# Four graph layers on one core: normalization, a mask and two additions move to GpSimd, ScalarE takes a copy from VectorE, and the target columns are spread by transposes

## The chip, the cores and the metric

The kernel runs on one core of a Trainium2 chip. The metric is the device time of one launch in microseconds; the profile is one execution of the program, and its clock column is the share of the full 2.4 GHz that TensorE was granted (0.5 is the 1.2 GHz level).

## The reference

The input is `x` (16 graphs of 512 nodes with 128 features) and `adj` (16 x 512 x 512 integers). Four layers follow each other, each of the form `x = x + layer(relu(layernorm(x)), adj)`.

```python
# layer 0: graph attention, one head
Wh = h @ W.T;  s1 = Wh @ a1;  s2 = Wh @ a2
e = where(adj == 0, -inf, leaky_relu(s1[:, None] + s2[None, :], 0.2))
att = where(adj == 0, 0, softmax(e));  out = att @ Wh
# layer 1: graph attention, four heads of 32 features, with a bias b
h = x @ W.T + b;  logits = leaky_relu(l_src[:, None] + l_dst[None, :], 0.2)   # per head
out = softmax(where(adj == 1, logits, -9e15)) @ h
# layer 2: alpha = sigmoid(where(adj == k, leaky_relu((h * a_k) @ h.T))), k = 1..4;  out = alpha @ h + bias
# layer 3: three steps of  m = h @ weight[i];  aggr = (adj != 0).T @ m;  h = gru_cell(aggr, h)
```

The layernorm has no scale or shift: `(x - mean) / sqrt(var + 1e-5)`.

## The kernel before

**Tiling and stages.** A graph is four chunks (`C = 4`) of 128 nodes. Rows lie on the partitions, so an attention row block is a tile of 128 x 512. The work of a graph is cut into steps of four lists: `A_STEPS` (layer 0), `L_STEPS` (layer 1 up to its probabilities), `B_STEPS` (the end of layer 1, and layer 2) and `C_STEPS` (layer 3). Each engine runs the steps of all 16 graphs in one order of its own. `in_order` sorts them by `BEGIN[stage][graph] + WHEN[engine][step]`, two tables of numbers written out in the file, so that stages of up to four graphs are interleaved on each engine. Inside an engine the order is fixed; between engines there are semaphores.

**Norms.** For each of four norms VectorE takes statistics (`stats`, `aggr`), and in `deviation_of` writes `minus_mean` (line 634) and `var_eps` (636, 638). GpSimd raises `var_eps` to the power -0.5 (`rstd`, line 363) and multiplies it with `minus_mean` (`shift`, 365). ScalarE applies both with a relu to each chunk (`norm`, line 394), and TensorE transposes the four chunks (`turn_rows`, 936) once all are there. ScalarE copies the transposed rows `hT` (399).

**Layer 0.** One 512-column product with `dst_rep` (the weight of the target term repeated over 128 columns) gives the target term of every node, spread over all partitions (`dst0`, 961). Four 1-column products give the source term (`src0`, 941), which VectorE scales into `s_lift` (682), and four of 128 columns give the values (`values0`, 941). All of them go through the same PSUM bank, `a_bank`, one after the other. VectorE makes the mask of 128 x 2048 (`mask0`, 678).

**Layer 1.** The same with four heads: `dst1` to `dst4` are 512-column products with `dst_rep` (1005), and the values and source terms come from four products of 132 columns (`values1`, 1013). VectorE adds the bias `b1_rows` on its way out of PSUM (739) and writes `s_lift` (741). For each of 16 head and chunk pairs VectorE takes a masked maximum (`n` steps, 642) and the logits (`v` steps, 663), ScalarE the exponential (460), TensorE four transposes (`q` steps, 948) and ScalarE their copy (468). After the aggregation (1040) VectorE scales the result (796) and adds it to `x1` (802).

**Queues.** GpSimd's queue issues the loads of `adj_h` and `edges`, SP's those of `x` and of the transposed adjacency, ScalarE's the store.

## Time and profile before

| | |
|---|---|
| median of 3 runs | 1065.93 us (1064.18 to 1067.51) |
| the profiled execution's own time | 1066.04 us |
| its span, from the first to the last instruction | 1063.9 us |
| granted clock, mean | 0.967 |
| TensorE matmul busy | 954.6 us, 90% of the span |
| VectorE busy | 892.3 us, 84% |
| ScalarE busy | 864.0 us, 81% |
| GpSimd busy | 132.6 us, 12% |

A share of busy time is a mean over the span, which has a fill of about 100 us at its start and a drain at its end in which one graph is alone. A matmul of fp32 operands has two records in the profile, a transpose has one.

### The profile page before, as it was taken

The numbers are of one execution on the slowest core, as the hardware profiler recorded it, in microseconds if no ns is written. First come the engines' busy times: TensorE is split into PE (matmuls) and PEld (weight loads), VectorE is DVE, ScalarE is ACT, GpSimd is POOL, SyncE is SP. The second block draws the span as 40 slices with busy tenths as digits, with TensorE's granted clock in tenths as the row PEclk, the third lists the DMA queues.
The fourth block names the chain that finished last, engine by engine and source line by source line (L and its number), as shares of the span: only waits on it lengthen the run. The fifth ranks groups of instructions, "written<-read, shape, count | busy, mean of one in ns | idle before, by whom it ended". The sixth has DMA issues, their size and how long they took to land.

```text
span 1063.9 us, 16086 instructions
## 1 busy us (share of the span) xinstructions
PE 954.6 (90%) x5024; PEld 609.6 (57%) x5024; DVE 892.3 (84%) x2710; ACT 864.0 (81%) x1860; POOL 132.6 (12%) x170
## 2 busy tenths in 40 slices
PE   4588998999989899999989899998989999998866
PEld 3455565666566566656556566656656665655443
DVE  5296989899898979899897989989897989979543
ACT  3367888979888897988888897988889798887742
POOL 1102011010202011020201201020201101010000
PEclk8558999999999999999999999999999999999989
DMA  2401204021210403121220402121030302111000
GB/s 72 109 1 39 72 11 109 11 61 52 68 51 14 106 11 77 44 60 51 56 64 10 110 11 60 60 61 51 15 105 11 79 31 61 50 40 51 1 11 10
DMA packets 42477, 52.32 MB, mean 49 GB/s; under 512 B 1296, under 2 KB 25872, under 8 KB 42384
## 3 DMA queue, kind: packets, MB, share of 16 engines
q0 software_dynamic: 16896, 25.17, 10.7%
q1 hardware_dynamic: 17040, 21.83, 6.5%
q10 hardware_dynamic: 8448, 4.20, 1.3%
q8 instruction: 44, 0.72, 0.3%
q14 instruction: 49, 0.40, 0.1%
HBM read 55.39 MB, written 4.19 MB: 56 GB/s over the span
## 4 chain that ended last, share of the span: by engine, by line
PE 52%; DVE 28%; ACT 10%; issue 6%; POOL 3%; DMA 0%; DVEq 0%; SPq 0%; ACTq 0%; POOLq 0%
PE l_bank L948 7%; DVE probs L642 6%; PE a_bank L981 6%; PE x_bank L1040 4%; PE a_bank L948 3%; PE h_bank L1102 3%; ACT hn L394 3%; PE r_bank L1102 3%; PE r_bank L1105 3%; DVE sess L843 3%; DVE sess L836 3%; PE h_bank L1105 3%; PE n_bank L1105 3%; DVE probs L663 3%; POOL rstd L363 2%
## 5 line engine op out<-in xcount | busy, mean ns | idle before, releaser
L663 DVE SCALAR_TENSOR_TENSOR probs<-spread,s_lift,probs 128x512 f32<-128x512 f32 x320 | 237.4, 747 | 4.0 <-DVE rmax L642 0.5
L642 DVE CUSTOM_DVE_ANT_0 probs<-spread,mask 128x512 f32<-128x512 f32 x320 | 211.8, 684 | 2.4 <-ACT spread L450 2.3
L363 POOL TENSOR_TENSOR rstd<-var_eps,power 128x4 f32<-128x4 f32 x64 | 88.0, 1375 | 882.5 <-DVE var_eps L636 603.0
L460 ACT ACTIVATE probs<-probs,shift_p 128x512 f32<-128x512 f32 x256 | 185.7, 725 | 5.7 <-DVE shift_p L659 5.7
L468 ACT ACTIVATE pT<-l_bank 128x512 f32<-128x512 f32 x256 | 151.8, 600 | 46.5 <-PE l_bank L948 46.3
L948 PEld LDWEIGHTS l_bank<-ident,probs 128*128 128x128 f32 x1024 | 124.3, 144 | 73.8 <-issue 46.0
L948 PE MATMUL l_bank<-ident,probs 128*128 128x128 f32 x1024 | 150.5, 278 | 6.1 <-ACT probs L460 5.1
L394 ACT ACTIVATE hn<-x,shift,rstd 128x128 f32<-128x128 f32 x192 | 80.5, 492 | 26.1 <-POOL shift L365 26.0
L1005 PE MATMUL l_bank<-hT,dst_rep 128*128 128x512 f32 x128 | 73.6, 658 | 12.1 <-ACT pT L468 8.5
L870 DVE SCALAR_TENSOR_TENSOR hid_n<-r_t,hid_n 128x512 f32<-128x512 f32 x48 | 33.1, 689 | 57.8 <-ACT r_t L518 57.8
L981 PE MATMUL a_bank<-values,pT 128*128 128x128 f32 x512 | 65.7, 286 | 0.7 <-ACT pT L428 0.7
L1088 PE MATMUL y_bank<-hn,sess 128*128 128x128 f32 x512 | 61.6, 278 | 4.2 <-DVE sess L843 4.1
L1088 PEld LDWEIGHTS y_bank<-hn,sess 128*128 128x128 f32 x512 | 58.4, 192 | 11.9 <-DVE sess L843 11.9
L981 PEld LDWEIGHTS a_bank<-values,pT 128*128 128x128 f32 x512 | 63.0, 202 | 2.0 <-ACT pT L428 2.0
L1040 PE MATMUL x_bank<-pT,values 128*32 128x512 f32 x512 | 58.2, 595 | 0.7 <-ACT pT L468 0.7
L450 ACT ACTIVATE spread<-l_bank 128x512 f32<-128x512 f32 x64 | 38.4, 600 | 23.4 <-PE l_bank L1005 23.4
L948 PEld LDWEIGHTS a_bank<-ident,probs 128*128 128x128 f32 x256 | 29.9, 149 | 44.5 <-ACT pT L428 35.8
L948 PE MATMUL a_bank<-ident,probs 128*128 128x128 f32 x256 | 44.4, 300 | 9.7 <-ACT probs L423 5.6
L460 ACT ACTIVATION_READ_ACCUMULATOR probs<-probs,shift_p 128x1 f32 x256 | 51.8, 202 | 0.0
L1105 PE MATMUL r_bank<-aggT,gi_w 128*128 128x512 f32 x96 | 49.4, 596 | 0.0
L1105 PE MATMUL h_bank<-aggT,gi_w 128*128 128x512 f32 x96 | 49.1, 593 | 0.0
L1105 PE MATMUL n_bank<-aggT,gi_w 128*128 128x512 f32 x96 | 49.1, 593 | 0.0
(175 smaller groups left out, 1956.5 us busy)
## 6 DMA issues: line engine op xcount, KB each, us to landing
adjt_i<-in_adj_t SPq DMA_DIRECT2D x16, 1024.0 KB, 5.2
edges<-in_adj POOLq DMA_DIRECT2D x16, 1024.0 KB, 5.9
adj_h<-in_adj POOLq DMA_DIRECT2D x16, 512.0 KB, 7.7
xin<-in_x SPq DMA_DIRECT2D x16, 256.0 KB, 2.9
out<-out_sb ACTq DMA_DIRECT2D x16, 256.0 KB, 3.8
weights_sb<-in_weights SPq DMA_DIRECT2D x1, 840.0 KB, 4.7
```

The source lines that it names most:

```text
L363: g.tensor_tensor(rstd[n][:], var_eps[n][:], power[:], op=ALU.pow).then_inc(pool_step[n], 1)
L394: s.activation(hn[n][:, c, :], rows[:, c, :], ACT.Relu, bias=shift[n][:, c:c + 1], scale=rstd[n][:, c:c + 1]).then_inc(hn_ready[n], 1)
L460: s.activation(row, row, ACT.Exp, bias=shift_p[:, head, c:c + 1], accum_out=den[:, head, c:c + 1]).then_inc(probs_ready, 1)
L468: s.activation(pT[:, head - 1, :, c * P:(c + 1) * P], l_banks[unit % 2][:, :].rearrange("p (j i) -> p j i", j=C), ACT.Copy).then_inc(pT_co ...
L642: return v.tensor_tensor_reduce(out=row, in0=spread_row, in1=mask, scale=1.0 / LIFT, scalar=-3e38, op0=ALU.subtract, op1=ALU.max, accum_ou ...
L663: v.scalar_tensor_tensor(row, spread_row, source, row, ALU.min, ALU.subtract, reverse1=True).then_inc(ready, 1)
L948: last = t.transpose(dst[:, j * P:(j + 1) * P], row[:, j * P:(j + 1) * P], ident[:])
L981: last = t.matmul(a_bank[:, c * P:(c + 1) * P], pT0[:, j, c * P:(c + 1) * P], values0[:, j, :], start=(j == 0), stop=(j == C - 1))
L1005: t.matmul(l_banks[head % 2][:, :], dst_rep[:, head, :], hT[1][:, :], start=True, stop=True).then_inc(dst_ready, 1)
L1040: last = t.matmul(x_bank[h * HD:(h + 1) * HD, :], values1[:, j, h * HD:(h + 1) * HD], pT[:, h, j, :], start=(j == 0), stop=(j == C - 1), s ...
L1088: last = t.matmul(y_bank[:, c * P:(c + 1) * P], sess[:, j, c * P:(c + 1) * P], hn[2][:, j, :], start=False, stop=(j == C - 1), skip_group_ ...
L1105: t.matmul(bank[:, :], gi_w[:, layer, gate * D:(gate + 1) * D], aggT[:, :], start=start, stop=True).then_inc(gi_ready, 1)
```

## The change

What it does, part by part:

- **Norms.** `minus_mean` and `shift` go. GpSimd writes each normalized chunk itself, `(x - mean) * rstd`, in sixteen instructions per graph of 128 x 128. The relu moves into the readers: ScalarE's copy of `hT`, ScalarE's `state_hi`, VectorE's `split`. For layer 2, whose product reads the rows untransposed, GpSimd runs one pass more over the 512 columns (`ramp2`), and the product waits for it. TensorE's transposes wait for one chunk at a time.
- **Layer 0.** The source and target terms become columns 128 and 129 of the values (`values0_w`, 130 columns). Four times 130 don't fit into a bank, so three chunks are multiplied and copied (`values0`), then the fourth (`last0`). The target column is then spread over the partitions by four transposes of the column repeated 128 times (`spread_column`) in place of the product with `dst_rep`. The order in `a_bank` becomes rows, values, last, dst. GpSimd makes the mask in four parts of 512 columns.
- **Layer 1.** `values1_w` has 136 columns (values, four source and four target terms). ScalarE copies them from PSUM in two instructions of 272 columns. VectorE adds a constant to the 16 source columns. `dst1` to `dst4` are `spread_column` too, and come after `values1`. The bias isn't added to the values any more: GpSimd adds it to `x1` after the norm has read that (`plus1`, 512 columns).
- **x2.** GpSimd adds `x1` to the scaled result (512 columns), between VectorE's `scaled` and `stats2`.
- **hTa.** ScalarE makes it from `hT` in SBUF in place of the PSUM bank.
- **Orders.** `BEGIN` and `WHEN` hold other numbers, so each engine has another order of steps. The distance between two graphs in `BEGIN` goes from about 6,780 to about 6,270.
- **GpSimd's queue.** The load of the next graph's `adj_h` now also waits for the mask parts of the graph before, and the mask parts stand behind that load.

```diff
-A_STEPS = (... + [f"norm0_{c}" for c in range(4)] + ["rows0", "mask0", "dst0", "src0", "values0"] + ...
+A_STEPS = (... + [f"norm0_{c}" for c in range(4)] + [f"mask0_{c}" for c in range(4)] + ["rows0", "values0", "last0", "dst0"] + ...
...
+    COLS0, COLS1 = D + 2, D + 2 * H1
+    SOURCE1, TARGET1 = D, D + H1
...
-                pool.wait_ge(pool_step[n], p.count(1, 1))
-                g.tensor_tensor(shift[n][:], minus_mean[n][:], rstd[n][:], op=ALU.mult).then_inc(ln_ready[n], 1)
+            def norm(p, n, c, rows):
+                if c == 0:
+                    pool.wait_ge(pool_step[n], p.count(1, 1))
+                    if p.before().exists():
+                        pool.wait_ge(hT_ready[n], p.before().count(1, 1))
+                g.tensor_scalar(hn[n][:, c, :], rows[:, c, :], moments[n][:, c, 0:1], rstd[n][:, c:c + 1],
+                                op0=ALU.subtract, op1=ALU.mult).then_inc(hn_ready[n], 1)
...
             def load_adj(p):
                 if p.before().exists():
+                    pool.wait_ge(mask0_ready, p.before().count(C, C))
...
+            def mask_of(p, c):
+                pool.wait_ge(adj_loaded, p.count(16, 16))
+                if p.before().exists():
+                    pool.wait_ge(logits0_ready, p.before().count(C, c + 1))
+                g.tensor_scalar(mask0[:, c, :], adj_h[:, c, :], 0.0, MASK, ALU.is_equal,
+                                ALU.mult).then_inc(mask0_ready, 1)
+            def plus_b1(p):
+                pool.wait_ge(hn_ready[1], p.count(C, C))
...
+                g.tensor_tensor(row, row, b1_rows[:, :].unsqueeze(1).to_broadcast([P, C, D]),
+                                op=ALU.add).then_inc(plus1_ready, 1)
...
+                if step == "x2":
+                    pool.wait_ge(scaled_ready, p.count(1, 1))
+                    pool.wait_ge(plus1_ready, p.count(1, 1))
+                    g.tensor_tensor(x2[:, :, :], x1[:, p.graph % 2, :, :], x2[:, :, :], op=ALU.add).then_inc(x2_ready, 1)
...
+                if step == "ramp2":
+                    pool.wait_ge(hT_ready[2], p.count(1, 1))
+                    g.tensor_scalar(hn[2][:, :, :], hn[2][:, :, :], 0.0, None, op0=ALU.max).then_inc(ramp_done, 1)
...
-                s.activation(hT[n][:, :], src[:, :], ACT.Copy).then_inc(hT_copied[n], 1)
+                s.activation(hT[n][:, :], src[:, :], ACT.Relu).then_inc(hT_copied[n], 1)
...
+                elif step == "last0":
+                    act.wait_ge(last0_ready, p.count(1, 1))
+                    s.activation(values0[:, C - 1, :], a_bank[:, 0:COLS0], ACT.Copy).then_inc(last0_copied, 1)
...
+                elif step == "values1":
+                    act.wait_ge(val1_ready, p.count(1, 1))
+                    if prev.exists():
+                        act.wait_ge(l1_done, prev.count(1, 1))
+                    for half in range(2):
+                        s.activation(values1[:, 2 * half:2 * half + 2, :].rearrange("p c k -> p (c k)"),
+                                     l_banks[half][:, 0:2 * COLS1], ACT.Copy).then_inc(val1_copied, 1)
...
-                        v.tensor_tensor(values1[:, pair, :], both[:, :, 0:D],
-                                        b1_rows[:, :].unsqueeze(1).to_broadcast([P, 2, D]), ALU.add)
+                    v.tensor_tensor(sources1[:, :, :], values1[:, :, SOURCE1:SOURCE1 + H1],
+                                    source_const[:, :].unsqueeze(1).to_broadcast([P, C, H1]),
+                                    ALU.add).then_inc(src1_copied, 1)
...
             def turn_rows(p, n, dst):
-                pe.wait_ge(hn_ready[n], p.count(C, C))
                 for c in range(C):
+                    pe.wait_ge(hn_ready[n], p.count(C, c + 1))
                     last = t.transpose(dst[:, c * P:(c + 1) * P], hn[n][:, c, :], ident[:])
...
+            def spread_column(dst, columns, k, ready):
                 for c in range(C):
+                    last = t.transpose(dst[:, c * P:(c + 1) * P], columns[:, c, k:k + 1].to_broadcast([P, P]), ident[:])
+                last.then_inc(ready, 1)
...
-                    t.matmul(l_banks[head % 2][:, :], dst_rep[:, head, :], hT[1][:, :], start=True,
-                             stop=True).then_inc(dst_ready, 1)
+                    spread_column(l_banks[head % 2], values1, TARGET1 + head - 1, dst_ready)
```

## Rows read from the trace of the kernel before

**Rows 1.** Stretches of the span: busy us of each engine, TensorE's clock, DMA.
```profile
149.49:757.01 607.52, 574.04 (x3135) 367.29 (x3138) 550.70 (x1672) 535.42 (x1161) 84.28 (x100) 1.00 0.20 53
...
106.00:172.00 66.00, 62.69 (x332) 39.29 (x331) 60.13 (x180) 59.10 (x130) 8.03 (x10) 1.00 0.24 60
964.00:1000.00 36.00, 30.68 (x171) 18.86 (x172) 26.41 (x68) 27.05 (x60) 1.75 (x2) 1.00 0.13 37
```

**Rows 2.** TensorE's waits, 149.49 to 757.01 us: total, times, longest.
```profile
PE a_bank L941 <- DVE s_lift L682: 13.6, 10, 1.4
PE x_bank L936 <- ACT hn L394: 8.9, 12, 0.8
```

**Rows 3.** The chain that ended last, 309.71 to 311.86 us: start, us, work.
```profile
309.71 0.86 PE r_bank L1102 x2
...
311.43 0.44 PE l_bank L948 x4
```

**Rows 4.** TensorE's groups, same ten periods: busy us, mean ns | idle before.
```profile
L948 PE MATMUL l_bank<-ident,probs 128*128 128x128 f32 x640 | 91.2, 273 | 0.2 <-ACT probs L460 0.2
...
L1005 PE MATMUL l_bank<-hT,dst_rep 128*128 128x512 f32 x80 | 43.1, 621 | 6.0 <-ACT pT L468 6.0
...
L961 PE MATMUL a_bank<-hT,dst_rep 128*128 128x512 f32 x20 | 10.2, 593 | 0.0
...
L941 PE MATMUL a_bank<-src_w,hT 128*128 128x1 f32 x80 | 9.5, 240 | 0.0
```

**Rows 5.** VectorE's groups that the change touches, same ten periods.
```profile
L739 DVE TENSOR_TENSOR values<-l_bank,b_rows 128x256 f32<-128x256 f32 x20 | 8.2, 413 | 0.0
...
L802 DVE TENSOR_TENSOR x<-x 128x512 f32<-128x512 f32 x10 | 6.9, 690 | 0.3
...
L678 DVE TENSOR_SCALAR mask<-adj_h 128x2048 bf16<-128x2048 bf16 x10 | 6.8, 684 | 0.0
...
L634 DVE TENSOR_SCALAR minus_mean<-moments 128x4 f32<-128x4 f32 x40 | 6.7, 167 | 0.7
```

**Rows 6.** ScalarE's groups: two of the ten periods, one of the whole span.
```profile
L394 ACT ACTIVATE hn<-x,shift,rstd 128x128 f32<-128x128 f32 x121 | 50.7, 493 | 3.4 <-POOL shift L365 3.3
...
L450 ACT ACTIVATE spread<-l_bank 128x512 f32<-128x512 f32 x40 | 24.1, 602 | 9.0 <-PE l_bank L1005 9.0
...
L535 ACT ACTIVATE gi_w<-r_bank 128x384 f32<-128x384 f32 x1 | 0.5, 491 | 0.7 <-PE r_bank L931 0.7
```

**Rows 7.** GpSimd's groups, whole span.
```profile
L365 POOL TENSOR_TENSOR shift<-minus_mean,rstd 128x4 f32<-128x4 f32 x64 | 19.4, 303 | 5.0
...
L358 POOL TENSOR_SCALAR_AFFINE_SELECT ident<-ident 128x128 f32<-128x128 f32 x1 | 0.3, 287 | 0.2 <-POOL ones_h L356 0.2
L352 POOL MEMSET ones<- 128x128 f32 x1 | 0.2, 205 | 0.3 <-POOLq L1175 0.3
...
L355 POOL MEMSET minus_half<- 128x1 f32 x1 | 0.1, 96 | 0.0
```

**Rows 8.** The power operation (ns least/median/most), one of them, VectorE beside it.
```profile
L363 POOL TENSOR_TENSOR rstd<-var_eps,power x64: 1007/1380/2586, 5.3 to 1022.5; 128x4 f32<-128x4 f32 x64
...
524.31 1.38 POOL L363 TENSOR_TENSOR rstd<-var_eps,power 128x4 f32<-128x4 f32 x1 [6.25 <-DVE var_eps L636]
...
524.14 0.68 DVE L642 CUSTOM_DVE_ANT_0 probs<-spread,mask 128x512 f32<-128x512 f32 x1
...
524.75 0.69 DVE L642 CUSTOM_DVE_ANT_0 probs<-spread,mask 128x512 f32<-128x512 f32 x1
```

**Rows 9.** VectorE's groups with two SBUF inputs, ten periods, first and last.
```profile
L663 DVE SCALAR_TENSOR_TENSOR probs<-spread,s_lift,probs 128x512 f32<-128x512 f32 x200 | 148.3, 747 | 2.5 <-DVE rmax L642 0.5
L642 DVE CUSTOM_DVE_ANT_0 probs<-spread,mask 128x512 f32<-128x512 f32 x200 | 132.2, 683 | 0.1
...
L836 DVE SCALAR_TENSOR_TENSOR sess<-sess 128x512 f32<-128x512 f32 x40 | 25.9, 686 | 0.3 <-ACT sess L488 0.2
...
L865 DVE TENSOR_TENSOR state_lo<-hn,state_hi 128x512 fp32r<-128x512 f32 x10 | 6.8, 684 | 0.0
```

More of the change, by code:

```diff
@@ L20 @@
 PLAIN = 1024.0
[L23 removed]
+A_STEPS = (["stats0", "aggr0", "mean0"] + [f"norm0_{c}" for c in range(4)] + [f"mask0_{c}" for c in range(4)] + ["rows0", "values0", "last0", "dst0"] + [f"m{c}" for c in range(4)]
            + ["u0", "top0", "u1", "t0", "below0", "u2", "t1", "max0", "u3", "t2", "t3", "den0", "rden0"] + [f"sum0_{c}" for c in range(4)] + ["x1"])
[L25 removed]
+L_STEPS = (["stats1", "aggr1", "mean1"] + [f"norm1_{c}" for c in range(4)] + ["plus1", "count", "rows1", "mask1", "edges", "values1", "dst1"]
            + [f"n{c}" for c in range(4)] + ["dst2"]
@@ L31 @@
 B_STEPS = ([f"sum1_{j}" for j in range(4)] + ["den1", "scaled", "x2", "stats2", "aggr2", "mean2"]
-           + [f"norm2_{c}" for c in range(4)] + ["rows2"] + [f"z{n}" for n in range(4)] + ["kinds"]
+           + [f"norm2_{c}" for c in range(4)] + ["rows2", "ramp2"] + [f"z{n}" for n in range(4)] + ["kinds"]
            + [f"s{n}" for n in range(4)] + [f"w{n}" for n in range(4)] + ["x3", "stats3", "aggr3", "mean3"]
@@ L220, in graph_layers @@
         moments = [sb(f"moments{n}", [P, C, 2]) for n in range(NORMS)]
-        var_eps, rstd, minus_mean, shift = ([sb(f"{m}{n}", [P, C]) for n in range(NORMS)]
-                                            for m in ("var_eps", "rstd", "minus_mean", "shift"))
+        var_eps, rstd = ([sb(f"{m}{n}", [P, C]) for n in range(NORMS)] for m in ("var_eps", "rstd"))
         cell = [sb(f"cell{n}", [P, 1]) for n in range(NORMS)]
@@ L280, in graph_layers @@
         pool_step = [sem(f"pool_step{n}") for n in range(NORMS)]
-        ln_ready = [sem(f"ln_ready{n}") for n in range(NORMS)]
         hn_ready = [sem(f"hn_ready{n}") for n in range(NORMS)]
@@ L381, in step_of @@
                     deviation(p, int(step[4]))
+                if step[:5] == "norm0":
+                    norm(p, 0, int(step[6]), xin[:, p.graph % 2, :, :])
+                if step[:5] == "norm1":
+                    norm(p, 1, int(step[6]), x1[:, p.graph % 2, :, :])
+                if step[:5] == "norm2":
+                    if step == "norm2_0" and p.before().exists():
+                        pool.wait_ge(av2_done, p.before().count(1, 1))
+                    norm(p, 2, int(step[6]), x2)
+                if step == "ramp2":
+                    pool.wait_ge(hT_ready[2], p.count(1, 1))
+                    g.tensor_scalar(hn[2][:, :, :], hn[2][:, :, :], 0.0, None, op0=ALU.max).then_inc(ramp_done, 1)
+                if step[:5] == "norm3":
+                    if step == "norm3_0" and p.before().exists():
+                        pool.wait_ge(rest_ready, p.before().count(LAYERS, 1))
+                    norm(p, 3, int(step[6]), x3)
             load_adj(Place(0))
@@ L432, in step_l @@
                 prev = p.before()
-                if step[:5] == "norm1":
-                    norm(p, 1, int(step[6]), x1[:, p.graph % 2, :, :])
-                elif step == "rows1":
+                if step == "rows1":
                     copy_hT(p, 1, l_bank0)
```

194 lines of the change are left out of this document (80 added, 114 removed), and 118 rows, old and new, of the table WHEN.

## The prediction

> **What bounds the kernel now.** The split of the span into stretches comes first [rows 1]. Ten whole periods lie between the starts of two layer 1 aggregations, at 149.49 and 757.01 us, so one graph takes 607.52 / 10 = 60.75 us. Of these TensorE is busy 57.40, VectorE 55.07, ScalarE 53.54 and GpSimd 8.43. Three engines are close to full; the reader is to see that TensorE has 3.35 us of room per graph, VectorE 5.68, and that the granted clock is 1.00 there (the 2.4 GHz level). Outside the window the kernel fills and drains.
>
> What TensorE waits for is in the table of waits of the same window [rows 2]: 13.6 us over ten graphs for the `s_lift` column of layer 0, 8.9 for normalized rows from ScalarE, the most of 33.5 us in all. So little is handed over, the rest is TensorE's own work: it is the first bound. VectorE at 91% is the second, and so near that relief for one alone would soon meet the other.
>
> **TensorE's part of the change.** The chain that ended last [rows 3] prices what is swapped. In the chain a 512-column matmul advances TensorE by 0.86 us (two passes, each a record), four transposes by 0.44 us when nothing holds them. The busy columns give the same order [rows 4]: a 512-wide `dst` product is 43.1 / 40 = 1.08 us in layer 1 and 10.2 / 10 = 1.02 in layer 0, four transposes 91.2 / 160 = 0.57. The change replaces five such products per graph (4.31 + 1.02 = 5.33 us) by five sets of four transposes of a repeated column. No row shows a repeated column as an input; bounds are 0.44 (the chain) and 1.08 (no gain), and I take 0.57, the row of the same operation: 2.85. It also drops the four source products of layer 0, 0.95 us. `values0` grows from 128 to 130 columns and `values1` from 132 to 136, in four products each: 24 columns at 0.86 us for 512, +0.04. Sum: 57.40 - 5.33 - 0.95 + 2.85 + 0.04 = 54.0, or 3.4 less per graph.
>
> The 1.36 us per graph that TensorE waits before `values0` goes with the source column. In its place come two waits of the same kind, on the copies before `last0` and before the `dst0` transposes, each behind a ScalarE copy of about 0.5 us. In TensorE's new order, as the tables sort it, `rows2`, `z0` and `q0` stand between `values0` and `last0`, and `z1` to `z3` and `q1` between `last0` and `dst0`, which covers them; but with ScalarE and VectorE nearer to each other other waits will come, and I keep the idle time at 3.35.
>
> **VectorE's part.** Per graph it loses [rows 5] the layer 0 mask 0.68, the layer 1 bias additions 0.82, the addition of x2 0.69, and seven small instructions of the size of `minus_mean`, 0.167 each (four of these, three of `s_lift`): 1.17. Such small ones advance the engine by less than they last, so 0.5 is the lower end of that term. It gains a 16-column addition, 0.17. Sum 3.36 - 0.17 = 3.2: 51.9 us. The split step changes from one two-input form to another of the same width: nothing.
>
> **ScalarE's part.** The norms take 50.7 / 121 = 0.42 us each [rows 6], sixteen of them 6.7 per graph. It gains two copies of 272 columns: 384 columns took 0.491 and 512 took 0.60, 0.85 ns per column, so 0.40 each and 0.79 together; the last copy of 130 columns is 0.28 by the same line, and `values0` with 390 columns saves 0.10. 53.54 - 6.7 + 0.97 = 47.8. It falls behind and is cover from now on.
>
> **GpSimd's part.** No row has such an operation at this width, so each is bounded [rows 7]. A 128-column write took 0.205 us and a 1-column one about 0.10; a 128-column pass with one input took 0.287. Sixteen norms of 128 columns lie between 0.205 and ScalarE's own 0.49; I take 0.29: 4.6 us. A 512-column pass with one input is 0.10 + 4 x 0.105 = 0.52 to 0.10 + 4 x 0.187 = 0.85; I take 0.6: four mask parts 2.4, `ramp2` (four times as wide in all, 512 columns) 0.6. Additions of 512 columns with two inputs lie between VectorE's 0.69 and 2 x 0.85 = 1.7; I take 1.2, twice 2.4. New work 10.0 us, less the four `shift` products of 0.3: GpSimd goes from 8.4 to about 17 of 60 us and is no bound by itself. The Trainium skill (GPSIMD Engine Reference, section Elementwise) gives about 2.6 cycles per element at 1.2 GHz for a two-input addition; an estimate by it is 1.1 us for 512 columns. No row here shows one, and by it the sum of new work would be 9.8.
>
> **What the new work meets.** This decides. The power operation, with two four-column inputs, took between 1.007 and 2.586 us, 1.380 in the median [rows 8]. One of the median length was issued at 524.31, just after a VectorE instruction with two SBUF inputs (spread and mask) had begun at 524.14 to last to 524.82. That its 0.37 us above the shortest ends about there says that GpSimd's reads were kept out until that instruction let go, and 2.586 that they can be kept out for two. The reverse doesn't show: VectorE's next one starts at 524.75, 0.61 after the last. But four-column reads are over at once, and those of the new work aren't. VectorE's instructions with two SBUF inputs are [rows 9] 148.3 + 132.2 us in the two softmax forms and 141 in eight further groups (the first 25.9, the last 6.8): 422 in 607.5 us, 69% of the time. If every GpSimd read of the new work holds VectorE for its whole duration, VectorE loses 10.0 x 0.69 = 6.9 us per graph; if none does, 0. A 128-column GpSimd write takes 0.1 us beyond its start, half of its duration; I take half as held, 3.5 us: VectorE at 51.9 + 3.5 = 55.4.
>
> **Sum.** The busier engine is then VectorE with 55.4 (TensorE 54.0), much as it was TensorE with 57.4 (VectorE 55.1), and I keep that idle of 3.35: 58.8 us per graph, 2.0 less. The stretch from 106 to 1000 us is worked at about this pace (its first and last windows still have TensorE busy for 62.69 of 66 and 30.68 of 36 us [rows 1]): 894 / 60.75 = 14.7 periods. In the fill and the drain one graph is alone; there a norm loses 0.30 of `shift` and four times 0.42 of ScalarE [rows 6, 7] and gains four times 0.29, while x2 costs 0.5 more and the first graph has one copy more: nothing on balance, 3 us either way. 14.7 x 2.0 = 29 us. The profiled execution's own time is 1066.04 for a span of 1063.9, and the median of the runs is 1065.93, the same within 0.1: 1066 - 29 = 1037 us.
>
> **Rivals.**
> 1. VectorE isn't held at all (the short reads slip into its gaps, as those of the power operation do). TensorE bounds again: 54.0 + 3.35 = 57.35, 3.4 less, 14.7 x 3.4 = 50: 1016 us. For it: VectorE's starts beside GpSimd today. Against: those reads are of four elements. Chance 0.24.
> 2. The other side: each GpSimd operation holds VectorE for its whole duration. VectorE 51.9 + 6.9 = 58.8, plus 3.35 is 62.2, 1.4 more than now: 1066 + 21 = 1087 us. With two-input additions at their upper bound of 1.7 it is 1097. It decides from the point where VectorE passes 57.4, a loss of 5.5 us per graph, 0.55 us for each us of new GpSimd work. For it: the durations of 1.38 and 2.59 us show that the two engines do exclude each other. Against: VectorE waits 5.7 us per graph anyway, and part of the loss falls there. The Trainium skill (SBUF, section Who interferes with whom) states this rule outright: the shared pair is held for the full instruction and the other blocks. This trace shows the block in one direction only. Chance 0.24.
> 3. The norms come late: kept out one VectorE instruction each, four take 4 x (0.68 + 0.29) = 3.9 us in place of 0.30 + 1.68 = 2.0, and x2 is 1.2 later; TensorE, in order, stands at the transposes of `rows2` and `rows3`. That is 2 x 1.9 + 1.2 = 5.0 us per graph, of which half beyond cover gives 54.0 + 3.35 + 2.5 = 59.9: 0.9 less, 1053 us. For it: TensorE waits 0.89 us per graph there already [rows 2]. Against: it now starts with the first norm. Chance 0.10.
> 4. The change doesn't cheapen the spreading (a repeated column costs a full product): TensorE 54.0 + 2.5 = 56.5, period 59.9 again, 1053 us. Nothing speaks for it but the missing row. Chance 0.04.
>
> **Numbers.** The forecast has 0.38, with its own range of 1024 to 1052. Within 0.3% (3 us, about what a measurement of this kernel tells from no change) lies only the seam between the forecast and rival 2: 0.06, taken from these two. Faster: 0.24 + 0.10 + 0.04 + 0.34 = 0.72; slower 0.22. Down to 1008 (rival 1 with transposes at 0.44) and up to 1086, with half of rival 2 beyond it, the range leaves out about 2 in 10.
>
> **What would show it.** Right: the sets of transposes for `dst` at about 0.57 us; TensorE at 54 and ScalarE at 48 us per period; GpSimd at 17 or more with waits in its durations; the softmax instructions of VectorE longer in the mean than 747 and 684 ns, or with gaps, by 3.5 us per graph in sum. Rival 1: these means unchanged and TensorE at 94% busy. Rival 2: VectorE at 58 us or more per period. Rival 3: VectorE and TensorE both under 90%, with waits on `hn` from GpSimd. Wrong in size it would be if a norm on GpSimd takes 0.5 us or more, or if the bound moves to GpSimd's queue, where mask parts wait for a load issued shortly before them.

## The result, and the profile after

The changed kernel takes 1203.2 us in the median of four runs (1202.1 to 1203.3), the kernel before 1065.1 beside it (1063.4 to 1067.5): 1.129 times as long, with a 95% interval of 1.127 to 1.132. The forecast was 1037, faster. The time lies outside the range, and past the rival of the other side (1087) too.

The page of the changed kernel, with the share of busy time, TensorE's clock and GpSimd's use in 40 slices:

```profile
span 1201.5 us, 16247 instructions
...
PE 982.3 (82%) x5056; PEld 638.3 (53%) x5056; DVE 901.4 (75%) x2545; ACT 788.7 (66%) x1652; POOL 579.9 (48%) x474
...
POOL 4427375482727547272753717365472727532120
PEclk8567898999988899998989989898999989898989
```

The longer span isn't filled with work. TensorE has 982.3 us of it and is idle for 219, where before it had 954.6 and was idle for 109. VectorE and ScalarE are idle too. No engine is a bound by its own work. GpSimd's row repeats: slices at 10 to 40% stand between slices at 50 to 90%, so its work comes in bursts.

Ten whole periods again, between the starts of two layer 1 aggregations (busy of TensorE, its weight loads, VectorE, ScalarE, GpSimd; clock, DMA share, GB/s), and in them TensorE's waits that answer to [rows 2] (total, times, longest):

```profile
160.46:859.38 698.92, 593.09 (x3152) 385.93 (x3151) 559.64 (x1575) 489.81 (x1031) 368.46 (x290) 0.94 0.18 46
```

```profile
PE x_bank L941 <- POOL hn L356: 57.4, 68, 3.4
...
PE a_bank L941 <- POOL hn L356: 2.6, 3, 0.9
```

A period is 69.9 us, where [rows 1] had 60.75. Of the 9.1 more, 1.9 are in TensorE's busy time (59.3 after 57.4) and 7.2 in its idle time (10.6 after 3.35). Waits for normalized rows are 6.0 us per graph; they were 0.89. VectorE at 56.0 and ScalarE at 49.0 are where the prediction had them (55.4 and 47.8).

GpSimd's groups over the whole span (busy, mean ns | idle before), and least, median and most of the two costliest:

```profile
L356 POOL TENSOR_SCALAR hn<-x,moments,rstd 128x128 f32<-128x128 f32 x192 | 197.1, 1037 | 6.9 <-issue 5.0
L370 POOL TENSOR_SCALAR mask<-adj_h 128x512 bf16<-128x512 bf16 x64 | 146.7, 2314 | 83.1 <-DMA adj_h<-in_adj 83.1
...
L408 POOL TENSOR_SCALAR hn<-hn 128x512 f32<-128x512 f32 x16 | 25.5, 1597 | 0.8 <-PE x_bank L941 0.5
L378 POOL TENSOR_TENSOR x<-x,b_rows 128x512 f32<-128x512 f32 x16 | 21.6, 1352 | 1.3
L385 POOL TENSOR_TENSOR x<-x 128x512 f32<-128x512 f32 x16 | 20.7, 1291 | 35.7 <-DVE x L804 35.7
```

```profile
L356 POOL TENSOR_SCALAR hn<-x,moments,rstd x192: 784/878/1942, 40.3 to 1162.1; 128x128 f32<-128x128 f32 x192
```

```profile
L370 POOL TENSOR_SCALAR mask<-adj_h x64: 1915/2248/3184, 9.9 to 1028.4; 128x512 bf16<-128x512 bf16 x64
```

None of these is near its price, the additions apart. A norm chunk takes 784 ns at least and 1037 in the mean, where 0.29 us was taken and 0.49 was the upper bound. A mask part takes 1915 at least against 0.6. The relu pass takes 1.6 us, and is one input with one operation, yet slower than the additions of two inputs.

What this does is to be seen on GpSimd's own timeline (start, us, work):

```profile
647.39 1.03 POOL L348 TENSOR_TENSOR rstd<-var_eps,power 128x4 f32<-128x4 f32 x1 [22.89 <-DVE var_eps L656]
648.53 3.20 POOL L356 TENSOR_SCALAR hn<-x,moments,rstd 128x128 f32<-128x128 f32 x4
651.82 1.29 POOL L378 TENSOR_TENSOR x<-x,b_rows 128x512 f32<-128x512 f32 x1
653.07 1.47 POOL L348 TENSOR_TENSOR rstd<-var_eps,power 128x4 f32<-128x4 f32 x1
654.64 3.67 POOL L356 TENSOR_SCALAR hn<-xin,moments,rstd 128x128 f32<-128x128 f32 x4
658.29 1.26 POOL L385 TENSOR_TENSOR x<-x 128x512 f32<-128x512 f32 x1
661.16 1.51 POOL L348 TENSOR_TENSOR rstd<-var_eps,power 128x4 f32<-128x4 f32 x1 [1.61 <-DVE var_eps L656]
662.84 4.56 POOL L356 TENSOR_SCALAR hn<-x,moments,rstd 128x128 f32<-128x128 f32 x4 [0.17 <-issue]
667.35 0.86 POOL L395 DMA_DIRECT2D edges<-in_adj  x1
668.21 0.75 POOL L364 DMA_DIRECT2D adj_h<-in_adj  x1
668.97 1.59 POOL L408 TENSOR_SCALAR hn<-hn 128x512 f32<-128x512 f32 x1
```

Three power operations start within 14 us, and the engine waits for 1.6 of the 23.2 us. Norm 2's power is made from 661.16 on; its fourth chunk is ready at 667.40, 6.2 us later. Before, power, shift and four chunks on ScalarE took 1.38 + 0.30 + 4 x 0.42 = 3.4 us [rows 6 to 8]. Then the layer 2 product waits for the relu pass, which stands behind two load issues and ends at 670.56.

The VectorE and TensorE groups that the forecast named:

```profile
L662 DVE CUSTOM_DVE_ANT_0 probs<-spread,mask 128x512 f32<-128x512 f32 x320 | 218.1, 702 | 11.4 <-ACT spread L434 7.0 <-ACT spread L481 3.7
L686 DVE SCALAR_TENSOR_TENSOR probs<-spread,sources,probs 128x512 f32<-128x512 f32 x256 | 194.6, 764 | 3.1
...
L946 PE MATMUL l_bank<-ident,values 128*128 128x128 f32 x256 | 41.4, 291 | 5.3 <-DVE other_kinds L754 2.9 <-ACT pT L499 2.4
```

Least, median and most of the masked maximum, in the changed kernel and before:

```profile
L662 DVE CUSTOM_DVE_ANT_0 probs<-spread,mask x320: 675/685/1093, 16.9 to 1111.8; 128x512 f32<-128x512 f32 x160
```

```profile
L642 DVE CUSTOM_DVE_ANT_0 probs<-spread,mask x320: 654/684/693, 18.0 to 981.2; 128x512 f32<-128x512 f32 x160
```

In the mean the masked maximum went from 684 to 702 ns and the logits from 747 to 764. The longest masked maximum takes 0.41 us more than the median, and the shortest norm chunk on GpSimd takes 0.78: no masked maximum was lengthened by a whole GpSimd instruction. A set of four transposes for `dst` costs 41.4 / 64 = 0.65 us of TensorE, close to the 0.57 taken.

### The profile page after: what moved, and what is told of

It is laid out like the page before. It is cut to its first block and busy times, and to the rows that moved or that the text cites. A ratio compares the mean times of both kernels' runs of the same rounds, so it can differ in the third digit from the quotient of the medians.

```text
span 1201.5 us, 16247 instructions
## 1 busy us (share of the span) xinstructions
PE 982.3 (82%) x5056; PEld 638.3 (53%) x5056; DVE 901.4 (75%) x2545; ACT 788.7 (66%) x1652; POOL 579.9 (48%) x474
## 5 line engine op out<-in xcount | busy, mean ns | idle before, releaser
L356 POOL TENSOR_SCALAR hn<-x,moments,rstd 128x128 f32<-128x128 f32 x192 | 197.1, 1037 | 6.9 <-issue 5.0
L686 DVE SCALAR_TENSOR_TENSOR probs<-spread,sources,probs 128x512 f32<-128x512 f32 x256 | 194.6, 764 | 3.1
L951 PE MATMUL l_bank<-ident,probs 128*128 128x128 f32 x1024 | 164.8, 291 | 32.2 <-ACT probs L491 30.8
L370 POOL TENSOR_SCALAR mask<-adj_h 128x512 bf16<-128x512 bf16 x64 | 146.7, 2314 | 83.1 <-DMA adj_h<-in_adj 83.1
L941 PE MATMUL x_bank<-ident,hn 128*128 128x128 f32 x128 | 48.6, 386 | 93.5 <-POOL hn L356 93.5
L941 PEld LDWEIGHTS x_bank<-ident,hn 128*128 128x128 f32 x128 | 20.2, 158 | 123.9 <-POOL hn L356 122.8
L1093 PEld LDWEIGHTS y_bank<-hn,sess 128*128 128x128 f32 x512 | 60.4, 191 | 24.3 <-DVE sess L848 24.2
L884 DVE SCALAR_TENSOR_TENSOR keep<-z_t,state 128x512 f32<-128x512 f32 x32 | 26.6, 831 | 44.2 <-ACT z_t L546 44.2
L356 POOL TENSOR_SCALAR hn<-xin,moments,rstd 128x128 f32<-128x128 f32 x64 | 57.5, 910 | 1.7
L644 DVE BATCH_NORM_STATS2 stats<-x 128x6 f32<-128x128 f32 x192 | 41.8, 281 | 18.7 <-POOL x L385 17.9
L535 ACT ACTIVATE aggT<-n_bank 128x512 f32<-128x512 f32 x32 | 19.1, 597 | 54.5 <-PE n_bank L1125 54.5
```

The costliest lines, as they stand in the source:

```text
L356: g.tensor_scalar(hn[n][:, c, :], rows[:, c, :], moments[n][:, c, 0:1], rstd[n][:, c:c + 1], op0=ALU.subtract, op1=ALU.mult).then_inc(hn_r ...
L370: g.tensor_scalar(mask0[:, c, :], adj_h[:, c, :], 0.0, MASK, ALU.is_equal, ALU.mult).then_inc(mask0_ready, 1)
L686: v.scalar_tensor_tensor(row, spread_row, source, row, ALU.min, ALU.subtract, reverse1=True).then_inc(ready, 1)
L941: last = t.transpose(dst[:, c * P:(c + 1) * P], hn[n][:, c, :], ident[:])
L951: last = t.transpose(dst[:, j * P:(j + 1) * P], row[:, j * P:(j + 1) * P], ident[:])
L1093: last = t.matmul(y_bank[:, c * P:(c + 1) * P], sess[:, j, c * P:(c + 1) * P], hn[2][:, j, :], start=False, stop=(j == C - 1), skip_group_ ...
```

## The experiments

Each median stands with its ratio to the kernel before, run beside it, and the 95% interval. Before each run two or more outcomes were written down, with a time for each. In nine of the eighteen (e1, e2, e3, e4, e7, e9, e10, e12, e15) the time fell outside all of them, in e3 and e15 by under 3 us.

### Undoing parts of the changed kernel

Five kernels keep the change and its new orders, and move work back. `ON_ACT` lists the norms that ScalarE makes as before.

```diff
+ON_ACT = (0, 1, 2, 3)      # e1;  (2, 3) in e2
+                if n in ON_ACT:
+                    pool.wait_ge(pool_step[n], p.count(1, 1))
+                    g.tensor_tensor(shift[n][:], minus_mean[n][:], rstd[n][:], op=ALU.mult).then_inc(ln_ready[n], 1)
+                    return
...
-                g.tensor_scalar(mask0[:, c, :], adj_h[:, c, :], 0.0, MASK, ALU.is_equal,      # e3
+                        v.tensor_scalar(mask0[:, :, :], adj_h[:, :, :], 0.0, MASK, ALU.is_equal,
```

> The changed kernel with all sixteen norm instructions per graph back on ScalarE (shift on GpSimd and minus_mean on VectorE again, no ramp2), placed in ScalarE's order just before the copy of the rows (layer 0's before the copy of layer 1's values of the graph before); everything else as changed. Late results (the chains wait for slow GpSimd instructions, 0.8 to 2 us for each norm where 0.29 was priced): 187 us lie between the measured 1203 and the 1016 that TensorE's own work would give, and most of it goes: 1030 to 1080 us. Held VectorE (each GpSimd instruction blocks VectorE's two-input ones): the norms are 255 of GpSimd's 580 busy us, so 40 to 45% of the 187 goes: about 1120 us, and VectorE's mean durations fall only in part.

> The changed kernel with only the norms of layers 2 and 3 back on ScalarE, those whose rows TensorE waits for in the changed kernel (93.5 us before the transposes into x_bank); layers 0 and 1 stay on GpSimd. Late results: nearly all of what moving all four back gives, within 15 us of it. Held VectorE: half of what moving all four back gives.

> The changed kernel with layer 0's mask back on VectorE, one instruction of 0.69 us just before the first masked maximum; the norms stay on GpSimd. The four mask parts take 9 us of GpSimd's queue per graph and wait for a load (83 us in all), with a later norm behind them. Late results through GpSimd's queue: 20 to 70 us faster than the changed kernel, 1135 to 1185. Late results through each norm's own length alone: no change or slower, 1200 to 1215, for VectorE has 11 us more. Held VectorE: 147 of 580 busy us go, so about a quarter of 187: 1155 us, with VectorE's mean durations back halfway.

Measured: all norms back 1184.0 us (1.111 [1.108, 1.114]), norms 2 and 3 alone back 1149.8 (1.082 [1.078, 1.086]), the mask back 1197.5 (1.124 [1.120, 1.128]). Norms 2 and 3 are worth 53 us; moving 0 and 1 as well takes 34 of them away again. The mask, a quarter of GpSimd's busy time, is worth 6, and the two intervals overlap. So in this kernel the amount of GpSimd work costs less than which results come late. That with all norms back 119 us stay was more than either expectation had, and called for the next two, in which mask, norms and x2 are back and only the bias addition stays on GpSimd (in e6 norms 0 and 1 too).

> The changed kernel's orders with nearly all of the GpSimd work back: norms on ScalarE, layer 0's mask and the last addition of x2 on VectorE; the bias addition stays on GpSimd, the transposes of repeated columns and ScalarE's copy of the values stay. If slow GpSimd work alone makes the loss (1150 us with the norms of layers 2 and 3 back): 1010 to 1060 us. If the new orders are bad in themselves, fitted to durations that the chip doesn't have: still above 1110 us.

> As the run before, but the norms of layers 0 and 1 stay on GpSimd, where nothing was seen to wait long for them. Slow GpSimd work alone: 1020 to 1080 us. Bad orders: above 1110 us, and within 30 us of the run with all four norms back, or faster than it, as the norms of layers 0 and 1 on ScalarE cost 34 us with these orders (1184 against 1150).

Measured: 1178.8 (1.106 [1.102, 1.109]) and 1136.3 (1.066 [1.063, 1.070]). With nearly all work back, e5 is still 113 us above the kernel before, and it is slower than e6, which has more moved. The new orders don't fit work that isn't where they were made for.

### The orders

The changed kernel's computation in the old tables, each new step in the place of the one that it replaces (`values0`, `last0`, `dst0` for `dst0`, `src0`, `values0`; `values1` ahead of `dst1`).

```diff
-BEGIN, WHEN = ...   # the tables of the changed kernel
+BEGIN, WHEN = ...   # the tables of the kernel before
+NEW = {"mask0": [], "dst0": ["values0"], "src0": ["last0"], "values0": ["dst0"], "dst1": [],
+       "values1": ["values1", "dst1"]}
```

> The same work as the first kernel of this job, in the order of the kernel before on every engine: each step where it stood, layer 1's values now in the place of its first target product and that one in the place of the values, layer 0's values, last chunk and target column in the places of target, source and values; the bias addition on GpSimd before the load of the edges. So only TensorE's part, the copy of the values by ScalarE and the bias on GpSimd are new. If TensorE's work bounds as it did, at 54.0 us per graph in place of 57.4: 1015 to 1045 us. If the orders matter little: within 15 us of the first kernel of this job.

> All work as changed (norms, mask parts, both additions and ramp2 on GpSimd), in the order of the kernel before: norms right behind their power operation, x2 before mean2, the mask parts behind ramp2 of two graphs before and the load. If the new orders make most of the loss: below 1130 us. If slow GpSimd work makes it: 1180 to 1260 us, since these orders were made without it.

Measured: e7, with norms, mask and x2 back, 1103.8 (1.034 [1.028, 1.040]); e8, with all work moved, 1208.4 (1.134 [1.128, 1.140]). The new tables are worth 5 us with the work moved, where the two intervals overlap, and cost 75 with it back. They are no cause of the loss; the work that moved costs 105 us in the old tables (e8 less e7). What is left in e7, 38 us, is the cheaper way to spread the target columns, with ScalarE's copies, the relu in the readers and the bias addition on GpSimd. TensorE's waits there, whole span:

```profile
PE a_bank L1057 <- ACT values L539: 34.9, 16, 2.7
PE l_bank L1057 <- DVE other_kinds L861: 21.7, 16, 2.2
```

TensorE now stands behind copies that ScalarE makes, 2.2 us per graph in layer 0, where the `s_lift` wait that went was 1.2 per graph over the whole span. In layer 1 it stands 1.4 us per graph before the first target column, which needs the copied values and a count from VectorE. That is so in the old tables. In the changed kernel, with its own tables, the two waits of layer 0 are almost gone (whole span):

```profile
PE a_bank L970 <- ACT values L439: 0.6, 1, 0.6
```

```profile
PE a_bank L946 <- ACT values L443: 0.4, 1, 0.4
```

### The kernel before, with one part of the change

```diff
 e9_old_dst234
-                    t.matmul(l_banks[head % 2][:, :], dst_rep[:, head, :], hT[1][:, :], start=True,
+                    if head > 1:
+                        spread_column(l_banks[head % 2], values1, D + head - 1, dst_ready)
 e11_old_layer0
+SLOTS = {"tensor": {"dst0": ["values0"], "src0": ["last0"], "values0": ["dst0"]},
+         "scalar": {"dst0": ["values0"], "src0": [], "values0": ["last0", "dst0"]}}
 e10_old_norms_pool (in e14_old_norms23_pool for n = 2, 3 alone)
-                g.tensor_tensor(shift[n][:], minus_mean[n][:], rstd[n][:], op=ALU.mult).then_inc(ln_ready[n], 1)
+                for c in range(C):
+                    g.tensor_scalar(hn[n][:, c, :], rows[:, c, :], moments[n][:, c, 0:1], rstd[n][:, c:c + 1],
+                                    op0=ALU.subtract, op1=ALU.mult).then_inc(hn_ready[n], 1)
 e12_old_mask_pool
+                for c in range(C):
+                    g.tensor_scalar(mask0[:, c, :], adj_h[:, c, :], 0.0, MASK, ALU.is_equal, ALU.mult)
```

> The kernel before with one part alone: layer 1's target columns 2 to 4 spread by four transposes each instead of a 512-column product (136-column values, the additions of VectorE 132 columns wide instead of 128); the first head keeps its product, no order changes, and no step waits for more than before. If the price of the transposes holds (0.57 us a set against 1.08) and TensorE is the bound: 3 x 0.5 = 1.5 us per graph, 1040 to 1050 us. If TensorE's clock falls as it waits more and takes the saving back: 1055 to 1068 us, with a mean clock below 0.967.

> The kernel before with one part alone: all norms on GpSimd (128-column instructions right behind the power operation, relu in the readers, ramp2), orders unchanged. A norm then takes 4 x 0.8 to 1.0 us in place of 0.3 + 1.7, at four places per graph, 1.5 to 2.5 us later each. Late results: 2 or 3 of the places are waited for, 5 us per graph: 1110 to 1150 us. If the GpSimd work were hidden behind other work: 1055 to 1075 us.

> The kernel before with one part alone: layer 0's values with 130 columns in two goes, the last chunk and the spreading of the target column behind them in the same bank, in the slots of the old target, source and value products. The serial use of the bank makes TensorE wait for a copy of about 0.5 us before the last chunk and 0.3 before the transposes: in the run with all work back in the old orders it waited 34.9 us in all for that. If these waits set the time: 1075 to 1100 us. If TensorE's saved products (1.0 us for the target, 0.95 for the sources, less 0.57) win: 1045 to 1060 us.

> The kernel before with one part alone: layer 0's mask in four parts on GpSimd, right behind the load of adj_h, orders unchanged. GpSimd was idle there for 18 us and the parts take 9 after 6 of the load. Nobody waits for them: what is left is what they hold VectorE, 9 us of GpSimd reading per graph: with the 80 us that 460 us of unawaited GpSimd work cost, 147 us of it cost 25 less 11 saved on VectorE: 1070 to 1085 us. If VectorE is held only by norm-like instructions: 1055 to 1066 us.

> The kernel before with only the norms of layers 2 and 3 (and ramp2) on GpSimd, orders unchanged. If the lateness of these two, whose rows TensorE and ScalarE wait for, makes most of the 88 us: 1125 to 1150 us. If each norm's GpSimd time costs alike through VectorE: half of it, about 1110 us.

| run | median, us | ratio and interval |
|---|---|---|
| e9, heads 2 to 4 spread by transposes | 1074.9 | 1.009 [1.007, 1.011] |
| e11, layer 0's order of the bank | 1077.5 | 1.012 [1.010, 1.014] |
| e12, mask parts on GpSimd | 1089.7 | 1.023 [1.020, 1.025] |
| e10, all norms on GpSimd | 1154.0 | 1.082 [1.080, 1.085] |
| e14, norms 2 and 3 on GpSimd | 1150.9 | 1.080 [1.079, 1.082] |

e9 decides whether TensorE was the bound. Its group of the new transposes (busy, mean ns | idle before):

```profile
L951 PE MATMUL l_bank<-ident,values 128*128 128x128 f32 x192 | 31.2, 286 | 11.1 <-ACT pT L469 8.8 <-DVE other_kinds L749 2.3
```

48 sets for 31.2 us, 0.65 each, where a product was 1.08 [rows 4]: TensorE has less to do, 944.2 us of busy time after 954.6, and the kernel is 0.9% slower. The time alone could still hide a gain that a lower clock takes back, since the mean clock is 0.957 after 0.967. A stretch of the same five periods at a clock of 1.00 in both kernels settles it, e9 first (cut at ScalarE's copies of the layer 1 results; TensorE's busy time is the first behind the length, the clock the last but two):

```profile
397.25:700.21 302.96, 280.94 (x1597) 184.99 (x1596) 274.72 (x833) 266.79 (x582) 40.92 (x49) 1.00 0.20 53
```

```profile
396.49:699.64 303.15, 286.76 (x1567) 183.79 (x1566) 274.64 (x833) 267.29 (x583) 40.93 (x49) 1.00 0.20 53
```

TensorE works 5.8 us less there, 1.2 per graph, and the stretch takes 303.0 us for 303.2: nothing is gained. TensorE's work was not what the period followed. Of the 9.8 us by which e9's span is longer, 5.9 stand in five other periods, of 61.8 to 62.3 us, where its clock is 0.97; before, at 1.00, those graphs took 60.4 to 61.1. Why the clock is lower there stays open.

e14 (with it come the relu pass and the product that waits for it) holds nearly all of e10: norms 2 and 3 cost 85 us, 0 and 1 another 3. TensorE's wait for their rows, whole span:

```profile
PE x_bank L952 <- POOL hn L377: 60.7, 85, 4.4
```

In e12 some 10 us of the 24 lie in the first graph: its layer 1 result is copied at 105.97 us in place of 96.40. GpSimd's timeline:

```profile
2.03 0.96 POOL L371 DMA_DIRECT2D adj_h<-in_adj  x1 [0.22 <-issue]
9.84 7.61 POOL L376 TENSOR_SCALAR mask<-adj_h 128x512 bf16<-128x512 bf16 x4 [6.85 <-DMA adj_h<-in_adj]
17.42 1.04 POOL L363 TENSOR_TENSOR rstd<-var_eps,power 128x4 f32<-128x4 f32 x1
```

The mask parts stand ahead of norm 0's power, which starts at 17.42 us; it started at 5.33 before. The changed kernel's own order has the norm first, at 6.4 us, so this part isn't in its time. The rest of e12's price goes with VectorE: it is busy for 902.8 us after 892.3, though 10.9 us of masks are gone, so 140 us more of GpSimd work lengthened its other instructions by 21.

The four parts add up to 9 + 11 + 24 + 88 = 132 us beside the 138 of the whole change. That they come so near is chance: the 10 us of the first graph are not in the changed kernel, and neither is e11's price. In e11 TensorE waits 39.8 us for ScalarE's copies of the values, in the changed kernel 1.0. What holds is the rank: the norms.

### GpSimd work that nobody waits for, and lateness without work

Does GpSimd cost by keeping others from SBUF, or by handing over late? e4 adds to the kernel before all the instructions of the change's kinds, on buffers of their own; e13 adds only the sixteen norm-like ones per graph. e17 adds no reads: one write of 2048 columns ahead of the `shift` of norms 2 and 3.

```diff
 e13_spare_norms (e4_before_spare: also the mask parts, two additions and a relu pass)
+                for c in range(DUMMY_NORMS[n]):
+                    spare_do(g.tensor_scalar(spare[:, c, :], spare_a[:, 0:P], spare_b[:, 0:1], spare_b[:, 1:2],
+                                             op0=ALU.subtract, op1=ALU.mult))
 e17_old_late23
+                if n > 1:
+                    g.memset(unread[:, :, :], 1.0).then_inc(unread_done, 1)
                 g.tensor_tensor(shift[n][:], minus_mean[n][:], rstd[n][:], op=ALU.mult).then_inc(ln_ready[n], 1)
```

> The kernel before, with GpSimd work added that nobody waits for and that computes nothing of the result: per graph 16 norm-like instructions of 128 columns, 4 mask-like ones of 512, two additions and a maximum of 512 columns, on tiles of their own, put behind the power operations where GpSimd was idle; some 25 us per graph. Late results: 1065 to 1080 us, since no chain runs through it. Held VectorE: up to 25 x 0.69 = 17 us of VectorE per graph, which has 5.7 to spare: 1180 to 1250 us, with the two softmax instructions 100 ns or more longer in the mean.

> The kernel before with the norm-like part of the unawaited GpSimd work alone: 16 instructions of 128 columns per graph, no mask-like ones, no additions, no maximum. All norms on GpSimd cost 88 us (1154 against 1066). If that is mostly VectorE held by the reads: 1110 to 1140 us here. If it is mostly the later rows for TensorE and ScalarE: 1068 to 1100 us here, the rest being lateness.

> The kernel before, with one write-only GpSimd instruction of 2048 columns (about 1.8 us, nothing reads its tile) between the power operation and the shift of the norms of layers 2 and 3: their rows come some 1.8 us later, as they do with norms on GpSimd, but nothing more is read from SBUF by GpSimd. If lateness makes the 85 us that the norms of layers 2 and 3 cost on GpSimd: 1110 to 1140 us (1.8 x 2 x 16 = 58 us and more). If held VectorE or ramp2 makes it: 1070 to 1085 us.

Measured: e4 1144.7 us (1.075 [1.073, 1.078]), e13 1092.6 (1.025 [1.024, 1.027]), e17 1132.6 (1.063 [1.061, 1.065]). First e17: the added write in GpSimd's groups; TensorE's wait for the rows of norms 2 and 3 (they alone go to `x_bank`) over the whole span; the busy times. Behind them the same wait in the kernel before.

```profile
L371 POOL MEMSET unread<- 128x2048 f32 x32 | 57.8, 1807 | 1.9
```

```profile
PE x_bank L944 <- ACT hn L402: 65.1, 31, 7.3
```

```profile
PE 978.8 (87%) x5024; PEld 631.0 (56%) x5024; DVE 898.0 (79%) x2710; ACT 868.6 (77%) x1860; POOL 187.5 (17%) x202
```

```profile
PE x_bank L936 <- ACT hn L394: 20.6, 21, 5.6
```

57.8 us of writing, 1.8 per norm, cost 68 us of time. TensorE's wait for rows grew by 44.5 us, from 20.6 to 65.1, and its busy time by 24.2, from 954.6 to 978.8, for the same instructions at a lower clock (mean 0.939 after 0.967): 68.7 together. No other norm is delayed: from the end of `var_eps` to the power it is 5.3 us in sum over all 64, 5.2 before. Over the whole kernel, a microsecond by which norms 2 and 3 come later costs 1.2. Part of that is the clock, as the same period shows, at 1.00 in e17 and before:

```profile
677.58:740.50 62.92, 57.38 (x315) 36.91 (x314) 55.20 (x166) 53.55 (x119) 10.25 (x12) 1.00 0.19 51
```

```profile
639.22:699.64 60.42, 57.43 (x315) 36.86 (x314) 54.98 (x166) 53.44 (x119) 6.75 (x10) 1.00 0.20 53
```

Here 3.6 us of writing cost 2.5, some 0.7 per microsecond, and the one other such period costs 2.4. In e17's other whole periods the clock is 0.95 to 0.97, and they are 3.5 to 5.5 us longer than before. VectorE is hardly touched by the write: 898.0 us of busy time after 892.3.

Then e4 and e13. Busy times of e13 and of e4:

```profile
PE 955.0 (87%) x5008; PEld 611.0 (56%) x5024; DVE 899.7 (82%) x2710; ACT 865.1 (79%) x1860; POOL 379.8 (35%) x429
```

```profile
PE 965.9 (85%) x5024; PEld 612.5 (54%) x5024; DVE 952.5 (84%) x2710; ACT 870.0 (76%) x1860; POOL 591.7 (52%) x541
```

e4 has 212 us more of GpSimd work than e13, and VectorE is busy for 52.8 us more with the same 2710 instructions; the time is 52 us longer. That is the hold, a quarter of the duration for these forms. In e13, 252 us of norm-like work made VectorE busy for only 7.4 us more than the 892.3 before. Its 27 us have another cause, which the spare work brought in without my meaning it:

```profile
220.38 8.39 POOL L400 TENSOR_SCALAR spare<-spare_a,spare_b 128x128 f32<-128x128 f32 x8
228.74 1.11 POOL L370 TENSOR_TENSOR rstd<-var_eps,power 128x4 f32<-128x4 f32 x1
```

The eight spare instructions behind norm 0 kept the power of a later norm waiting, here from 225.3 (the end of its `var_eps` on VectorE) to 228.7. Twelve of the 64 powers started late so, by 32 us in sum. e13 is therefore no clean measure of the hold; only its difference to e4, which has the same late powers (33 us), is one.

### Relief

Two engines relieved without moving anything, and the mask on a third. e15 makes the layer 0 mask for the first graph only; e16 makes ScalarE's count pass for the first graph only; e18 gives the mask to ScalarE. e15's output is not the reference's.

```diff
 e15_old_less_vector
+                    if not prev.exists():
                         v.tensor_scalar(mask0[:, :, :], adj_h[:, :, :], 0.0, MASK, ALU.is_equal,
 e16_old_less_scalar
+                    if not prev.exists():
                         s.activation(counted[:, :, :], adj_h[:, :, :], ACT.Abs, bias=minus_half[:, 0:1],
 e18_old_mask_scalar
+                    s.activation(mask0[:, :, :], adj_h[:, :, :], ACT.Relu, bias=mask_bias[:, 0:1], scale=-MASK)
```

> The kernel before with layer 0's mask computed for the first graph alone and used for all (the output differs from the reference's): VectorE loses 0.69 us per graph, TensorE and ScalarE nothing. TensorE's saved 1.2 us per graph bought nothing. If VectorE in its fixed order is the bound: 0.5 to 0.7 us per graph, 1055 to 1059 us. If the time is set by a chain through several engines that doesn't pass this place: 1063 to 1067 us.

> The kernel before with the counting pass of ScalarE (2.0 us and the read of its sum) run for the first graph alone: ScalarE loses 2.2 us per graph. If VectorE is the bound: 1060 to 1067 us. If ScalarE in its fixed order sets the time: 1033 to 1045 us.

> The kernel before with layer 0's mask made by ScalarE (relu of 2^56 minus 2^56 times adj, one instruction of 2048 columns, 2.0 us) before its copy of layer 0's values, and not by VectorE. Taking 2.2 us off ScalarE changed nothing and taking 0.69 off VectorE gave 5 us. If ScalarE has that much room in its fixed order too: 1058 to 1063 us, faster than before. If 2 us more on ScalarE come late there: 1068 to 1090 us.

Measured: e15 1060.5 us (0.995 [0.994, 0.997]), e16 1065.8 (1.000 [0.999, 1.001]), e18 1082.0 (1.017 [1.015, 1.019]). Taking 8.0 us of busy time from VectorE gives 5.1 back, taking 28.9 from ScalarE gives nothing, taking 10.4 from TensorE (e9) costs 8.8. Moving the mask from VectorE to ScalarE, whose busy time grows by 26.6 us, costs 17. No experiment that computes the whole reference beat the kernel before.

## Why the prediction was wrong, point by point

**"It is the first bound": the step that failed first.** I read 94% busy and little handed over ("the rest is TensorE's own work") as TensorE bounding the period. e9 refutes it: with 1.2 us less TensorE work per graph, at the same clock, five periods take as long as before. ScalarE is no bound either (e16). VectorE's work does count: 8.0 us less gave 5.1 (e15), and 52.8 us more cost 52 (e4 less e13). But the changed kernel has only 9 us more of it, for 138 of time. What the period follows is a handing over between engines in fixed orders that passes through norms 2 and 3: e17 delays no other norm, and 57.8 us of delay cost 68. Which instructions close that loop, from layer 3 of one graph to the next, stays open. The row to have distrusted was in [rows 2]: twelve waits for `hn` of 0.8 us at most say that TensorE reaches those transposes just as the rows come. A wait that short on a result with nothing to spare is no sign of cover. e17 bears this out: with 1.8 us of delay at each of these norms the wait grew by 44.5 of 57.8 us.

**GpSimd's prices: mis-sized.** Taken 0.29, 0.6, 0.6 and 1.2 us; measured in the mean 1.04 (0.91 for norm 0), 2.3, 1.6 and 1.3. GpSimd went to 579.9 / 16 = 36 us per graph, not 17. The lower rows that I scaled from were writes and a one-operation pass; the upper bound for a norm, ScalarE's 0.49, had nothing to do with GpSimd. The sentence "wrong in size if a norm on GpSimd takes 0.5 us or more" holds.

**"I take half as held": VectorE's time was right by luck, and not what decided.** VectorE was forecast at 55.4 per period and has 56.0. The forecast added 3.5 us for 10.0 us of new GpSimd work; the measured 56.0 lies 4.1 above the same 51.9, for 28.4 us of it (36.8 after 8.4). Too little work and too large a share cancelled. Rival 2's mechanism is refuted: whole durations held would have made e4's 460 us of GpSimd work cost VectorE 0.69 x 460 = 317 us of busy time, and it cost 60. The Trainium skill (SBUF, section Who interferes with whom) has the pair held for the full instruction; the runs show a quarter of it for the 512-column forms, and for the norm-like form 7.4 of 252 us.

**"I keep that idle of 3.35": failed.** It is 10.6 us per graph, and the waits for `hn` are 6.0 of it.

**Rival 3, norms that come late: the right mechanism, priced too low.** It had 5.0 us of lateness per graph. By the means above it is 2 x (4.2 - 2.0) + 1.6 for the relu pass + 0.6 for x2 = 6.6, not far off. But it counted half of that, and took it from a period that cheaper transposes had shortened. At e17's rate of 1.18 per us, 6.6 us over 16 graphs would be 125 us, of the 138 measured. This is an estimate, and too high a one: in e14 a norm chunk takes 1.17 us in the mean, so its two norms are 2 x (4.7 - 2.0) = 5.4 us late, 102 us at that rate before the relu pass is counted, and e14 costs 85. What is shown is these 85 us for norms 2 and 3 alone. How the rest of the 138 divides among mask, waits of VectorE and ScalarE and the lower clock is not shown.

**TensorE's part: the price of a set near, the gain not.** Rival 4 falls: a set costs 0.65 us for 1.08. But 59.3 us busy per period stand against the forecast 54.0. With only the bias addition left on GpSimd (e7) TensorE is at 933.6 us, 1.3 less per graph than before, not 3.4; each of these kernels has a lower mean clock than the 0.967 before, 0.945 in e7, 0.957 in e9, 0.912 in the changed kernel. I had counted the clock as given.

**The two waits behind ScalarE's copies: rightly taken as covered.** In the changed kernel they are 1.0 us over the whole span. In the old tables they are not covered, 39.8 us in e11, which is a price of that order.

**The orders: put at nothing, and with the work moved that holds.** The changed kernel is 5 us faster in the new tables than in the old, hardly more than the noise.

## What to carry to other kernels

An engine at 94% is not the bound until relief for it has been seen to shorten the period: look for results that are consumed the moment they are made, with short waits that recur in most periods, and price a change first by how much later it makes these. Move work off a full engine only onto one whose price for that very form of instruction is in a trace, and keep it out of the stretch between a reduction and the matmul that waits for it. An order written for one set of durations is part of the tuning: swap it with the work, and measure it both ways.

## What the runs showed of the hardware

- **GpSimd's prices by form.** The least durations: 784 ns for two operations with a scalar per partition over 128 fp32 columns, 1915 for two operations over 512 bf16 columns, 1496 for a maximum over 512 fp32 columns, 1257 for an addition of two 512-column fp32 inputs, 1804 for a write of 2048 columns. Over 512 columns the one-input forms are the slower ones. The Trainium skill (GPSIMD Engine Reference, section Elementwise) gives about 2.6 cycles per element for the addition, by estimate 1.1 us here, which 1.257 bears out within 14%; its note (section Engine selection) that one-input work runs at about line rate is not borne out by the mask parts and the relu pass, which take longer than that addition.
- **A pair that holds each other in part.** 212 us more of GpSimd work with 512-column forms made VectorE busy for 53 us more; 252 us of the 128-column form for 7 us more. The longest masked maximum of the changed kernel takes 1093 ns, where the median is 685.
- **TensorE's clock can be lost behind a wait.** Three stretches of the changed kernel (TensorE's busy time first, the clock last but two):

```profile
616.00:624.00 8.00, 2.83 (x16) 1.75 (x15) 6.35 (x22) 4.48 (x11) 5.83 (x5) 0.88 0.43 131
624.00:632.00 8.00, 7.70 (x27) 5.50 (x27) 6.77 (x20) 5.08 (x12) 0.50 (x1) 0.69 0.00 0
632.00:640.00 8.00, 8.00 (x52) 5.72 (x51) 6.86 (x18) 7.83 (x18) 0.00 (x0) 1.00 0.00 0
```

TensorE has 2.83 us of work in the eight from 616, while it waits for norm 3, and in the next eight, in which it is full, the granted clock is 0.69 in the mean, between the 1.2 and the 2.4 GHz level. Then it is 1.00 again. So this wait is paid twice: once idle, once in slow matmuls. e17 prices it, 44.5 us of waits and 24.2 of slower work.
